# Exponential of a unit's second half in two instructions, with the scores behind each: a decoder layer on one core

## The reference, cut to what matters

```python
C_q = Q @ Wq_d
C_kv = K @ Wkv_d
CqWqk = (C_q @ W_qk).reshape(b, n, H, LKV)
scores = jnp.einsum('bnhl,bkl->bhnk', CqWqk, C_kv) / jnp.sqrt(LKV)
attn = jax.nn.softmax(scores, axis=-1)
V_up = (C_kv @ Wv_u).reshape(b, nkv, H, HD)
out = jnp.einsum('bhnk,bkhd->bnhd', attn, V_up)
```

## Time and profile before

| | |
|---|---|
| median of 3 runs | 2870.88 us |
| the profiled execution | 2869.99 us |
| its span | 2868.2 us, 1.8 us less |
| attention stage, about 389 to 1512 us of the span | 1123.5 us |
| mean granted TensorE clock | 0.97 of full speed |

### The profile page before, as it was taken

The page is one execution under the profiler, slowest core; times in us unless marked ns, Lnnn a source line. Parts: engine busy times, 40 slices in busy tenths (PEclk is TensorE's granted clock), DMA queues, the critical chain, the costliest instruction groups (busy, mean ns, idle before and its releaser), DMA issues. The chain is left out here.

```text
span 2868.2 us, 41196 instructions
## 1 busy us (share of the span) xinstructions
PE 2641.2 (92%) x14360; PEld 1991.5 (69%) x14360; DVE 2264.7 (79%) x2125; ACT 1671.0 (58%) x2611; POOL 1941.8 (68%) x1423
## 2 busy tenths in 40 slices
PE   6777889999999999999994999999999999999997
PEld 3545566666666666666663788888888888788885
DVE  1536668888888888778872799999999899899988
ACT  2242467777777777777773544454455554545553
POOL 1000347768776877677762888888887788888883
PEclk9979999999999999999996999999999999999999
DMA  7304567667667876687665123222222322132221
GB/s 263 130 18 171 179 218 215 201 185 237 198 208 210 258 209 206 197 251 212 196 200 212 52 89 110 81 67 74 76 72 80 119 74 88 67 118 81 74 96 74
DMA packets 166768, 420.60 MB, mean 147 GB/s; under 512 B 30113, under 2 KB 57634, under 8 KB 166050
## 3 DMA queue, kind: packets, MB, share of 16 engines
q1 hardware_dynamic: 161698, 407.93, 45.5%
q10 hardware_dynamic: 4864, 10.03, 0.9%
HBM read 248.43 MB, written 75.04 MB: 113 GB/s over the span
## 5 line engine op out<-in xcount | busy, mean ns | idle before, releaser
L1541 DVE SCALAR_TENSOR_TENSOR c_acc<-c_ps,c_sd,c_acc 128x1024 f32<-128x1024 f32 x448 | 573.3, 1282 | 96.9 <-PE c_ps L1398 96.8
L1150 POOL COPY b_pt<-b_tn 32x640 f32<-32x640 f32 x640 | 458.3, 716 | 270.6 <-DVE b_tn L1058 238.9
L1453 ACT ACTIVATE c_scaled<-c_ps,c_sgu 128x1024 f32<-128x1024 f32 x336 | 375.6, 1118 | 424.7 <-PE c_ps L1398 422.2
L1052 DVE TENSOR_REDUCE b_nm<-b_sc 128x1 f32<-128x1604 f32 x256 | 468.2, 1829 | 186.7 <-PE b_sc L889 185.1
L971 ACT ACTIVATE b_pr<-b_sc,b_nm 128x799 f32<-128x799 f32 (+1 forms) x512 | 477.0, 934 | 236.5 <-DVE b_nm L1052 212.6
L1624 POOL TENSOR_TENSOR c_sum_u<-c_sum_u,c_scaled 128x1024 f32<-128x1024 f32 x168 | 405.1, 2411 | 132.3 <-ACT c_scaled L1453 131.8
L1624 POOL TENSOR_TENSOR c_sum_g<-c_sum_g,c_scaled 128x1024 f32<-128x1024 f32 x168 | 405.0, 2411 | 82.6 <-ACT c_scaled L1453 82.4
L889 PE MATMUL b_sc<-b_kh,b_qs 128*128 128x402 f32 (+1 forms) x1024 | 403.3, 394 | 41.5 <-ACT b_pr L971 37.8
L908 PE MATMUL b_po<-b_pt,shared 128*64 128x256 f32 x2560 | 392.9, 395 | 25.3 <-DMA b_pt<-b_tn 25.0
L1058 DVE STREAM_TRANSPOSE b_tn<-b_pr 128x1280 f32<-128x1280 f32 x256 | 384.8, 1503 | 2.7 <-ACT b_pr L971 1.0
L889 PE MATMUL b_sc<-b_kl,b_qs 128*128 128x402 f32 (+1 forms) x1024 | 357.0, 349 | 0.0
(11 more groups left out here) (192 smaller groups left out, 4375.2 us busy)
## 6 DMA issues: line engine op xcount, KB each, us to landing
b_pt<-b_tn SPq DMA_DIRECT2D x1152, 80.0 KB, 2.6
c_uw_int<-wint_u SPq DMA_DIRECT2D x56, 512.0 KB, 3.4
c_gw_int<-wint_g SPq DMA_DIRECT2D x56, 512.0 KB, 3.4
c_dw_int<-wint_d SPq DMA_DIRECT2D x56, 512.0 KB, 3.4
a_cx<-in_b_ctxT SPq DMA_DIRECT2D x16, 1608.0 KB, 11.1
b_rw<-in_c_gw SPq DMA_DIRECT2D x28, 512.0 KB, 4.2
b_rz<-in_c_gz SPq DMA_DIRECT2D x28, 512.0 KB, 5.4
b_rw<-in_c_uw SPq DMA_DIRECT2D x28, 512.0 KB, 4.2
```

The costliest lines, as they stand in the source:

```text
L1052: V.tensor_reduce(nm[:, u % 2:u % 2 + 1], both, AXY, ALU.max, negate=True).then_inc(s_nm, 1)
L1150: G.tensor_copy(pt[s][32 * c:32 * c + 32, a, :, :], tn[s][32 * a:32 * a + 32, c, :, :]).then_inc(s_block, 1)
L1453: S.activation(dst[:, :], pair[SLOT[x, t] % 4][:, :], ACT.Identity, scale=scale(x, t)).then_inc(s_e, 1)
L1541: V.scalar_tensor_tensor(out=total, in0=pair[SLOT[x, t] % 4][:, :], scalar=scale(x, t), in1=total, op0=ALU.mult, op1=ALU.add).then_inc(s_a ...
```

## The change

The second half's exponential is issued as two activations, one for each PSUM bank: 398 columns, then 401. Each raises `s_ex`, so a unit now counts three. In the second half's scores the first chunk waits for the first of them (of the unit before), and the second chunk for the second. `den` holds three sums for each unit, in another layout, and GpSimd adds them in two additions, the second of which waits for the first. The other waits on `s_ex` and `s_sm` are counted anew and ask for the same work as before.

```diff
+EXPS = [[(110, 912, 0, 802, 2)], [(114, 512, 802, 1200, 0), (512, 913, 1200, NKV, 1)]]
...
-        den = sb("b_den", [P, 2, QT, 2])
+        den = sb("b_den", [P, 2, 3, QT])
...
-                if half and u:
-                    T.wait_ge(s_ex, 2 * u - 1)
-                elif u >= 2:
-                    T.wait_ge(s_ex, 2 * u - 2)
-                for k0, n, col in SCORE[half]:
+                if half == 0 and u >= 2:
+                    T.wait_ge(s_ex, 3 * u - 3)
+                for c, (k0, n, col) in enumerate(SCORE[half]):
+                    if half and u:
+                        T.wait_ge(s_ex, 3 * u - 2 + c)
...
-                T.wait_ge(s_ex, 2 * u + 2)
+                T.wait_ge(s_ex, 3 * u + 3)
...
-                        S.wait_ge(s_sm, g - 1)
+                        S.wait_ge(s_sm, 2 * g - 2)
...
-                S.activation(pr[u % 2][:, k0:k1], sc[:, at + lo:at + hi], ACT.Exp, bias=nm[:, u % 2:u % 2 + 1],
-                             accum_out=den[:, g % 2, q, half:half + 1]).then_inc(s_ex, 1)
+                for lo, hi, k0, k1, c in EXPS[half]:
+                    S.activation(pr[u % 2][:, k0:k1], sc[:, at + lo:at + hi], ACT.Exp, bias=nm[:, u % 2:u % 2 + 1],
+                                 accum_out=den[:, g % 2, c, q:q + 1]).then_inc(s_ex, 1)
...
-                G.wait_ge(s_ex, (g + 1) * UNITS * 2)
+                G.wait_ge(s_ex, (g + 1) * UNITS * 3)
...
-                G.tensor_tensor(rd[:, g % 2, :], den[:, g % 2, :, 0], den[:, g % 2, :, 1], ALU.add).then_inc(s_sm, 1)
+                G.tensor_tensor(rd[:, g % 2, :], den[:, g % 2, 0, :], den[:, g % 2, 1, :], ALU.add).then_inc(s_sm, 1)
+                G.wait_ge(s_sm, 2 * g + 1)
+                G.tensor_tensor(rd[:, g % 2, :], rd[:, g % 2, :], den[:, g % 2, 2, :], ALU.add).then_inc(s_sm, 1)
```

More of the change, by code:

```diff
@@ L961, in exponent @@
                 g, q = u // UNITS, u % UNITS
-                lo, hi, k0, k1 = SIDE[half]
                 at = half_at(u, half)
@@ L1049, in maximum @@
                 if u >= 2:
-                    V.wait_ge(s_ex, 2 * u - 2)
+                    V.wait_ge(s_ex, 3 * u - 3)
                 both = bass.AP(sc, min(first, second), [[3 * 1024, P], [abs(second - first), 2], [1, 802]])
@@ L1054, in turn @@
             def turn(u):
-                V.wait_ge(s_ex, 2 * u + 2)
+                V.wait_ge(s_ex, 3 * u + 3)
                 if u >= 4 and u % 2 == 0:
@@ L1060, in output @@
             def output(g):
-                V.wait_ge(s_sm, g + 1)
+                V.wait_ge(s_sm, 2 * g + 2)
                 V.reciprocal(rd[:, g % 2, :], rd[:, g % 2, :]).then_inc(s_rd, 1)
```

## The result

The changed kernel takes 2878.55 us (median of 13 runs), and 13 runs of the kernel before beside them 2871.61. The ratio is 1.0021, with a 95% interval of 1.0012 to 1.0030: slower by 6 us, more or less 2.6. The single runs of the kernel before reach from 2865.24 to 2878.23. The profiled execution took 2878.55 us, its span 2876.8.

What follows compares the result with a forecast made beforehand. Bound by the ring maximum, exponential, scores in somewhat over half of the units, TensorE's queue in the others. 0.17 us times 31 turns = 5.3, plus 1.5 for sums, gave 7 us more: 2878, range 2856 to 2888.

Steps and rivals of the forecast that it cites:

- The price of a half: ScalarE's second-half exponential: about 0.60 us for 398 columns, so a pair costs 0.25 us more than one instruction.
- rival A: ScalarE's queue before the exponentials of steps 0 and 4: a pair costs only 0.12 more, giving 2852 us; chance 0.18.
- The gain of the ring: Loop of maximum, exponential and scores: first score pair released 0.33 us earlier, but only 0.11 gained, 3.95 for 4.05.
- exponential 1: Second-half exponential in step 1 of the 8-unit turn, forecast 8.01 us after that of step 7, 8.11 before.
- The loss at the projection and the outputs: Steps 4 to 7: projection 0.25 us late behind ScalarE's copy, output products 0.37 late in all.
- One sign: TensorE's wait before the projection was to grow from 0.2 to above 0.6 us.
- The turn: Eight units of the attention loop, carried through in time: 0.37 lost less 0.21 gained, 0.17 us longer.
- The sums: GpSimd's 64 more additions of 0.199 us and a wait, delaying the exchange: 1.5 us taken, 6 if all showed.
- clean turn: One 8-unit turn without irregular waits, 444 to 479 us; its 0.17 us loss times 31 turns gave 5.3.
- C: Slower by more, 2884 to 2888: sums show 6 us, or the pair's surcharge is 0.28; chance 0.50 with the main case.
- Rival B: No change, 2871 within 5 us: the exchange's late transfers set the cadence, taking gains and hiding part of losses; chance 0.32.
- Its other form: TensorE's restart before the second score pair costs less than 0.29 us, so loss and gain cancel; within the same 0.32.

Runs made afterwards that it cites:

- copies' exchange: In step 4 of 8, ScalarE copies the turned probabilities ahead of the weighed latent: ratio 0.9990 in the kernel before, 0.9988 in the changed kernel.
- without the weights: Feed-forward weight preparation left out of the attention stage; stretch from first to last maximum 1095.3 us in the kernel before, 1102.7 in the changed kernel.
- step 4 unsplit: Changed kernel with the second half's exponential split only in units 0 and 1 modulo 8: 2874.13 us, ratio 1.0011.
- the split alone: Changed kernel, but the first pair of scores also waits for both exponentials: 2904.48 us, ratio 1.0112.
- two kernels: Changed kernel, and the one with only units 0 and 1 modulo 8 split, both with ScalarE's copies exchanged in step 4: ratios 0.9988 and 0.9992.

## Why the prediction was right

The forecast was 2878, the result 2878.55; over its own kernel before, 7 us against 6.9.

- **The price of a half**, 0.60 each and 0.25 for the pair: measured 0.593 and 0.590, and 0.24. The row of 0.688 at 512 columns with a bias tile was the right neighbour, and rival A's 0.404 row was not. The estimate from the figures of the Trainium skill (ScalarE: Activation LUTs, What ACT_TABLE_LOAD costs), 0.612 for 398 columns, is 0.02 above the measured 0.593.
- **The gain of the ring**, 0.11 for 0.33 of earlier release: exponential 1 follows exponential 0 in 3.92 (500.92 less 497.00), where 3.94 was forecast (8.01 less 4.07) and 4.06 stood before. TensorE's pause before the second pair is in its row at 498.31.
- **The loss at the projection and the outputs**: 0.25 at the projection and 0.35 in all at the output products, as in the table (forecast 0.25 and 0.37). That the copies' exchange brings a gain does not show this loss by itself, since it also helps kernels whose exponential of step 4 is whole. The comparison without the weights does: the same edit brings 12.0 us in the changed kernel (1102.7 to 1090.7) and 4.9 with step 4 unsplit (1090.3 to 1085.4). The 7.1 us between them are what the split costs there, 0.23 a turn; by the middle turns it is 0.30 (0.42 less 0.12). One sign was a little off: TensorE's wait ahead of the projection grew from 0.20 to 0.56, not to above 0.6.
- **The turn**: the times in the two tables came out within 0.04 us.
- **The sums**, 1.5 us: no run shows this term. Without the second addition the ratio was 1.0025 against 1.0021, and the stretch 2.3 us shorter in one execution.

What the sum left out. It multiplied a clean turn by 31. In six turns step 3 turns latent keys ahead of the weighing, and this waits for the copy of the turned probabilities too, which in step 2 follows both exponentials. The first such step in the kernel before and after, from the first scores of step 3 to those of the next (timelines of TensorE's weight loads); before:

```profile
504.98 0.19 PEld L889 LDWEIGHTS b_sc<-b_kh,b_qs 128*128 128x128 f32 x1
...
506.10 0.96 PEld L862 LDWEIGHTS b_mi<-ident,shared 64*32 64x32 f32 x64 [0.45 <-issue]
...
510.09 0.19 PEld L889 LDWEIGHTS b_sc<-b_kh,b_qs 128*128 128x128 f32 x1
```

After:

```profile
506.21 0.19 PEld L890 LDWEIGHTS b_sc<-b_kh,b_qs 128*128 128x128 f32 x1
...
507.65 0.96 PEld L863 LDWEIGHTS b_mi<-ident,shared 64*32 64x32 f32 x64 [0.77 <-issue]
...
511.64 0.19 PEld L890 LDWEIGHTS b_sc<-b_kh,b_qs 128*128 128x128 f32 x1
```

The step is 0.32 longer (5.43 for 5.11). What it adds to a whole turn is read from the starts of the maximum in step 7 without the weights, a clean turn first and then the first one with a latent turn. Kernel before:

```profile
461.08 1.83 DVE L1047 TENSOR_REDUCE b_nm<-b_sc 128x1 f32<-128x1604 f32 x1 [0.58 <-PE b_sc L884]
...
494.94 1.83 DVE L1047 TENSOR_REDUCE b_nm<-b_sc 128x1 f32<-128x1604 f32 x1 [0.60 <-PE b_sc L884]
...
529.84 1.83 DVE L1047 TENSOR_REDUCE b_nm<-b_sc 128x1 f32<-128x1604 f32 x1 [0.59 <-PE b_sc L884]
```

Changed kernel:

```profile
459.73 1.83 DVE L1048 TENSOR_REDUCE b_nm<-b_sc 128x1 f32<-128x1604 f32 x1 [0.72 <-PE b_sc L885]
...
493.79 1.83 DVE L1048 TENSOR_REDUCE b_nm<-b_sc 128x1 f32<-128x1604 f32 x1 [0.74 <-PE b_sc L885]
...
529.21 1.83 DVE L1048 TENSOR_REDUCE b_nm<-b_sc 128x1 f32<-128x1604 f32 x1 [0.71 <-PE b_sc L885]
```

The change adds 0.20 to the clean turn (34.06 for 33.86) and 0.52 to the other (35.42 for 34.90). Over the six such turns it adds 0.47 to 0.51 in unrounded times, which is 0.3 each over the clean turn, 1.8 us together. Then 0.17 times 31 is 5.3, and with 1.8 it is 7.1, against 7.4 measured without weights. So the 2878 owes something to luck: 1.5 us stood in the sum for additions that no run shows, and about 1.8 us for the latent turns were missing.

Rival A fell with the 0.59 of its halves, and C with the run without the second addition and the measured 0.24 for a pair, where it asked for 6 us from the sums or for 0.28. Rival B, the exchange as the pace, was half right. It does not hide the change's loss, since that loss is there with the weights (8.1 us of stretch) and without (7.4). But it hides gains: the kernels that should have been 6 to 12 us faster are not. Its other form, a pause of TensorE cheaper than 0.29 so that loss and gain cancel, is answered by the 0.20 a turn. Had the change been a real gain in the ring, my method would have promised too much.

## What to carry to other kernels

Splitting an instruction to release its consumer earlier costs its fixed part again, and the split stands in the same ring as the wait that it shortens; here 0.24 us bought half of the scores 0.33 earlier, and the ring was 0.13 shorter. Follow the added time down the producer's queue to every other engine that waits there, in the special steps too: the projection, the output products and six latent turns gave more away than the ring gained. Where a second helper, here an exchange beside other transfers, is already late in a third of the cases, a loss shows in full and a gain does not.

## What had not been expected of the hardware

With the split alone, the weighing's waits for the exchange fell by 24 us (43.8 to 19.5) while the ring slowed down, and the stretch grew by 31.5 us where the clean turns alone would have made it 42. And two kernels whose stretches without the weights are 4.6 and 9.9 us under that of the kernel before came out at 0.9988 and 0.9992 of its time with them, which a measurement cannot tell apart.
